# Two adaLN transformer layers on one core: statistics, normalisations, first weights and the mask of the wide attention moved

## The reference

```
mod = silu(c) @ wmod            # sa, ca, ga, sb, cb, gb: six vectors of 256 per layer
# layer 0
h = layernorm(x) * (1 + ca) + sa
x = x + ga * (softmax(q(h) k / 4) v @ Wo.T)       # 16 heads x 16, 4096 keys
h = layernorm(x) * (1 + cb) + sb
x = x + gb * experts(h)                           # 8 experts, top 2, hidden 64
# layer 1
h = layernorm(x) * (1 + ca) + sa
x = x + ga * (attention(h) @ Wproj.T + bproj)     # 16 heads x 16, 1024 keys
h = layernorm(x) * (1 + cb) + sb
h = h + causal_attention(rmsnorm(h, ln1_w)) @ wo  # 16 heads x 128
r = rmsnorm(h, ln2_w)
f = h + experts(r) + shared(r)                    # 16 experts of 176, top 6; shared 352
x = x + gb * f
```

## Time and profile before

| | |
|---|---|
| runs, us | 1858.6, 1856.21, 1847.71; median 1856.21 |
| the profiled execution, us | 1849.89, its span 1848.1 |
| TensorE busy | 1741.0 us, 94% of the span |
| VectorE busy | 1374.4 us, 74% |
| ScalarE busy | 1102.7 us, 60% |
| GpSimd busy | 517.1 us, 28% |

### The profile page before, as it was taken

The page is one execution under the profiler, slowest core; times in us unless marked ns, Lnnn a source line. Parts: engine busy times, 40 slices in busy tenths (PEclk is TensorE's granted clock), DMA queues, the critical chain, the costliest instruction groups (busy, mean ns, idle before and its releaser), DMA issues. The chain is left out here.

```text
span 1848.1 us, 29387 instructions
## 1 busy us (share of the span) xinstructions
PE 1741.0 (94%) x10457; PEld 1054.8 (57%) x10460; DVE 1374.4 (74%) x1911; ACT 1102.7 (60%) x2201; POOL 517.1 (28%) x527
## 2 busy tenths in 40 slices
PE   6999999999999999889999959999999999789997
PEld 4433333333333333564444448888888888678885
DVE  4799999999999997367999666666666666556666
ACT  2488888788788887455888425454545454244442
POOL 7247333333334522012323221110211020022223
PEclk7699999999999999999999989999999999989998
DMA  7122332223322300103546110000000000043331
GB/s 169 23 43 57 56 52 47 44 43 69 80 45 55 68 24 10 35 18 62 117 112 158 36 44 16 9 23 14 23 9 23 14 11 1 10 121 113 107 117 54
DMA packets 50606, 98.62 MB, mean 53 GB/s; under 512 B 11545, under 2 KB 21881, under 8 KB 48971
## 3 DMA queue, kind: packets, MB, share of 16 engines
q1 hardware_dynamic: 50219, 96.83, 22.0%
q10 hardware_dynamic: 288, 0.49, 0.2%
HBM read 65.63 MB, written 15.92 MB: 44 GB/s over the span
## 5 line engine op out<-in xcount | busy, mean ns | idle before, releaser
L726 DVE TENSOR_REDUCE a_max_part<-psum 128x1 f32<-128x1024 f32 x640 | 753.5, 1218 | 84.1 <-PE psum L614 82.3
L797 ACT ACTIVATE a_probs<-psum 128x512 f32<-128x512 f32 x1280 | 671.7, 600 | 186.3 <-PE psum L665 185.7
L665 PE MATMUL psum<-a_q_max,a_k_rows 51*128 51x512 f32 x1280 | 462.0, 449 | 3.4 <-ACT a_probs L797 1.8
L665 PEld LDWEIGHTS psum<-a_q_max,a_k_rows 51*128 51x128 f32 x1280 | 212.3, 187 | 354.2 <-ACT a_probs L797 286.7
L614 PE MATMUL psum<-a_k_rows,a_q_rows 48*128 48x512 f32 x1280 | 356.1, 472 | 13.7 <-DVE a_max_part L726 4.6
L654 PE MATMUL psum<-a_probs,a_v_ext 128*32 128x512 f32 x2560 | 343.3, 609 | 0.0
L614 PEld LDWEIGHTS psum<-a_k_rows,a_q_rows 48*128 48x128 f32 x1280 | 154.4, 189 | 86.7 <-DVE a_max_part L726 67.8
L1951 PE MATMUL psum<-high_t_parts,high_gu 128*128 128x512 f32 x600 | 146.4, 394 | 6.8 <-DVE high_t_parts L2045 6.8
L544 POOL TENSOR_TENSOR a_max_bf<-a_neg_max,a_zeros 128x8 bf16<-128x8 f32 x64 | 14.6, 229 | 472.5 <-issue 415.4
L417 POOL TENSOR_TENSOR a_k_rows<-a_k_in,a_k_rows 16x2048 fp32r<-16x2048 f32 x32 | 145.8, 4556 | 2.5
L1951 PEld LDWEIGHTS psum<-high_t_parts,high_gu 128*128 128x128 f32 x600 | 114.3, 191 | 31.5 <-issue 7.3
(11 more groups left out here) (223 smaller groups left out, 2139.2 us busy)
## 6 DMA issues: line engine op xcount, KB each, us to landing
o<-a_o_out SPq DMA_DIRECT2D x56, 256.0 KB, 2.2
a_k_in<-in_k SPq DMA_DIRECT2D x96, 128.0 KB, 4.6
a_q_rows<-q_high SPq DMA_DIRECT2D x124, 64.0 KB, 2.4
gu_in<-in_w_gu SPq DMA_DIRECT2D x25, 256.0 KB, 2.9
high_cw<-cw SPq DMA_DIRECT2D x24, 256.0 KB, 3.9
a_v_in<-in_v SPq DMA_DIRECT2D x16, 256.0 KB, 5.9
a_o<-o SPq DMA_DIRECT2D x8, 512.0 KB, 4.6
qk_in<-in_wqk SPq DMA_DIRECT2D x16, 256.0 KB, 2.7
```

What stands on the lines that cost most here:

```text
L665: pe.matmul(psum[:, self.bank_of(self.filling(j)), :], k_rows[rows, b, k0:k0 + P], self.q_max[rows, u % 2, :], start=True, stop=True).then ...
L726: dve.tensor_reduce(self.max_part[:, u % 2, c // self.nch, c % self.nch:c % self.nch + 1], psum[:, 2 * (n % 2):2 * (n % 2) + 2, :], AX.XY, ...
L797: act.activation(self.probs[:, p % self.pring, :], psum[:, self.bank_of(self.filling(j)), :], ACT.Exp).then_inc(self.exp_done, 1)
```

## The change

- `Attention` gets its statistics from `Merge.statistics`: behind add_out of steps 12 and 13 bn_stats of two tiles each, behind 16 to 19 of one each, into a tensor `stats` that lives through the kernel. `experts_low` does the same behind its additions. `normalise` with `stats` leaves out its bn_stats; its dummy matmuls stay.
- "n3" goes. `wide_attention` does both norms in its own block: aggregates, 16 scalar_tensor_tensor, squares with a sum on ScalarE in place of the second bn_stats, normalised tiles on VectorE (even) and ScalarE (odd), transposes, and the split parts straight from PSUM. TensorE issues 180 dummy matmuls before and 20 after the transposes.
- `WideWeights`: the first weights of the wide attention are loaded by SyncE at u = 6 and 17 of a1 and split by GpSimd at u = 13, 14, 15, 20 and 21.
- The mask is added by VectorE, in PSUM, before each maximum; the mask matmul and the bf16 casts go.
- The attention's prologue: queries and keys are sent separately (`load_q`, `load_kr`), the queries after `queries_done`; in a1 the Exp table is loaded first, and the query rows are cleared first; two value products are made ahead of the scores; 8 dummy matmuls stand on either side of `turn_maxima(0)`; in a0 75 follow the projections (`stay_busy`).
- `Front`: x is loaded before the first part of wmod; the rest of wmod waits for the first keys; 90 dummy matmuls at the start and 20 behind the column products.

The diff, cut:

```
+    def statistics(self, dve, k, stats):
+        i = k - self.PAIRS
+        tiles = (2 * i, 2 * i + 1) if 0 <= i < 2 else (i,) if i >= 4 else ()
+        for t in tiles:
+            dve.wait_ge(self.out_free, k + 1)
+            dve.bn_stats(stats[:, t, :], self.x[:, t, :]).then_inc(self.stats_done, 1)
...
                         for k in self.steps_after(u, s // 2):
                             merge.add_out(dve, k)
+                            merge.statistics(dve, k, stats)
...
             for k in range(in_slots, merge.STEPS):
                 merge.add_out(dve, k)
+                merge.statistics(dve, k, stats)
...
+                if weights is not None and u == 6:
+                    weights.load_first(sp)
+                if weights is not None and u == 17:
+                    weights.load_second(sp)
...
+                if weights is not None and u in (13, 14, 15):
+                    weights.split_first(pool, u - 13)
+                if weights is not None and u in (20, 21):
+                    weights.split_first(pool, u - 17)
...
             projection.products(pe, front)
+            if front is not None:
+                front.stay_busy(pe)
+            values_ahead = min(2, projection.tiles)
+            for t in range(values_ahead):
+                projection.value_products(pe, t)
...
+            keep_busy(pe, psum, self.ident_bf, 8)
             turn_maxima(0)
+            keep_busy(pe, psum, self.ident_bf, 8)
...
+            if not raw:
+                load_table()
+            projection.high_queries(act)
+            projection.queries_done(act)
             act.wait_ge(self.q_set, 1)
+            load_q(act, (1,), q_rows[:, 0, :], 0, self.q_loaded[0])
             if not raw:
+                projection.high_keys(act)
+                projection.chunk_done(act, 0)
                 act.wait_ge(self.k_set, 1)
...
+                load_kr(act, (1,), k_rows[:, 0, :], 0, self.q_loaded[0])
             projection.high_parts(act, 1)
+            if raw:
+                load_table()
...
-            sp.dma_start(self.wmod[:, 0, :, 0:first], by_row[0][:, :, 0:first]).then_inc(self.w_loaded[0], 16)
             for n in range(2):
                 sp.dma_start(self.x[:, 4 * n:4 * n + 4, :], x_tiles[:, 4 * n:4 * n + 4, :]).then_inc(self.x_loaded[n], 16)
+            sp.dma_start(self.wmod[:, 0, :, 0:first], by_row[0][:, :, 0:first]).then_inc(self.w_loaded[0], 16)
...
+            sp.wait_ge(attention.k_loaded, 96)
...
+            pe.wait_ge(self.ones_ready, 1)
+            keep_busy(pe, self.psum, self.ones_bf, 90)
...
+    def stay_busy(self, pe):
+        keep_busy(pe, self.psum, self.ones_bf, 75, 3)
...
+                if not made:
+                    for t in range(TT - 1):
+                        dve.bn_stats(stats[:, t, :], src[:, t, :]).then_inc(steps, 1)
+                    step(dve.bn_stats(stats[:, TT - 1, :], src[:, TT - 1, :]), TT)
...
             low(TT - 1)
+            for i in range(TT // 2 - 1):
+                statistics(i)
             add_pair(TT // 2 - 1)
-            dve.wait_ge(x_done, TT // 2)
+            statistics(TT // 2 - 1)
...
+        if n == 0:
+            pool.memset(self.zero[:, :], 0.0).then_inc(self.zero_set, 1)
+            pool.wait_ge(self.zero_set, 1)
+            pool.wait_ge(self.first_loaded, 48)
+        if n == 3:
+            pool.wait_ge(self.second_loaded, 32)
...
+        pool.tensor_tensor(parts[:, par, 0, :], src[:, :], self.zero[:, :].broadcast_to([P, size]), ALU.add).then_inc(self.high, 1)
+        pool.wait_ge(self.high, n + 1)
+        pool.tensor_tensor(parts[:, par, 1, :], src[:, :], parts[:, par, 0, :], ALU.subtract).then_inc(self.low, 1)
...
-                pe.matmul(s[:, i * P:n], id_bf[:, :], mask_bf[:, :], start=False, stop=True).then_inc(sc_full, 1)
+                mm.then_inc(sc_full, 1)
...
+            keep_busy(pe, psum, ident_bf, 180)
...
+                act.activation(junk[:, t % 2, :], x2[:, t, :], ACT.Square, accum_out=squares[:, t:t + 1]).then_inc(squared, 1)
...
+                    act.activation(t_parts[:, 0, c, half * 512:(half + 1) * 512], psum[:, 2 * c + half, :], ACT.Copy,
+                                   scale=scale_col[:, c:c + 1]).then_inc(t_hi, 1)
...
+                    last = bank_pair(i)[:, i * P:(i + 1) * P]
+                    dve.tensor_tensor(last, last, mask[:, :], ALU.add).then_inc(masked, 1)
+                    dve.wait_ge(masked, it * (2 * slots) + (slots * h + i + 1))
...
+            for t in range(TT):
+                dve.bn_aggr(mv[:, t, :], stats[:, t, :]).then_inc(steps, 1)
...
+            for t in range(0, TT, 2):
+                dve.tensor_scalar(xn[:, t, :], x2[:, t, :], rstd[:, 1, t:t + 1], None, ALU.mult).then_inc(even_ready, 1)
...
+                    dve.scalar_tensor_tensor(t_parts[:, 1, c, cut], psum[:, 2 * c + half, :], scale_col[:, c:c + 1], t_parts[:, 0, c, cut],
+                                             ALU.mult, ALU.subtract).then_inc(t_lo, 1)
...
-            dve.tensor_copy(mask_bf[:, :], mask[:, :]).then_inc(const_ready, 1)
-            dve.tensor_copy(id_bf[:, :], ident[:, :]).then_inc(const_ready, 1)
```

More of the change, by code:

```diff
@@ L456, in _, with run @@
             pool.memset(self.zeros[:, :], 0.0).then_inc(self.zeros_ready, 1)
+            self.clear_queries(pool)
             pool.memset(self.k_rows[:, :, :].bitcast(F32), 1.0).then_inc(self.k_set, 1)
             self.clear(pool)
[L460 removed]
+    def run(self, block, load_q, load_kr, q_loads, merge, projection, stats, front=None, weights=None):
         psum, nkt, nb, steps, groups, group, us = self.psum, self.nkt, self.nb, self.steps, self.groups, self.group, self.us
@@ L1075, in step, with statistics @@
                 dve.wait_ge(steps, done[0])
-            def statistics(src, rms, eps, nth):
-                for t in range(TT - 1):
-                    dve.bn_stats(stats[:, t, :], src[:, t, :]).then_inc(steps, 1)
-                step(dve.bn_stats(stats[:, TT - 1, :], src[:, TT - 1, :]), TT)
+            def statistics(src, eps):
+                if not made:
+                    for t in range(TT - 1):
+                        dve.bn_stats(stats[:, t, :], src[:, t, :]).then_inc(steps, 1)
+                    step(dve.bn_stats(stats[:, TT - 1, :], src[:, TT - 1, :]), TT)
                 for t in range(TT - 1):
@@ L2102, in adaln_two_layers @@
                     front.register(block, attention, i["c"], i["wmod"], i["ident"], i["x"], i["ln_w"], ln_w[:, :], chunks(i["wq0"]))
-                    attention.run(block, load_q, 6, merge, projection, front)
+                    attention.run(block, load_q, None, 6, merge, projection, stats, front)
         with ExitStack() as part:
```

248 lines of the change are left out of this document (155 added, 93 removed).

## The result

The changed kernel takes 1845.13 us in the median (1839.09 to 1852.63, 20 runs), the kernel before 1855.93 (1847.71 to 1861.41, 20 runs): the ratio is 0.9946, with a 95% interval of 0.9934 to 0.9957. That is 10 us by the ratio and 10.8 by the medians, a little over half a per cent, where 22 were forecast. The profiled execution of the changed kernel has a span of 1839.5 us against 1848.1, so 8.6 us less; the two profiles can be set side by side.

A forecast was written before the change was run, and what follows sets the result against it. It took TensorE to bound the loops, but not the seams between them. Terms summed to -17.3 us, 1832.6 for a profiled execution like that of before; the forecast median was 1834, 22 under that of before, range 1819 to 1851.

The forecast's parts named there:

- step 4: Narrow attention: wide weights' splits on GpSimd meet the maxima twice, 1.3 us each, plus 0.2 for loads: +2.8 (0 to +5).
- Step 1: End of first attention: moved statistics lengthen VectorE's tail by 1.75, transposes save 0.75: +1.0 us (0 to +1.8).
- the third rival: Seams: longer idle time of TensorE lets the clock fall, 1.7 us for each of two seams: 1840; chance 0.22.
- Step 2: End of the low experts: moved statistics add 1.6, transposes save 0.75: +0.85 us (-0.7 to +1.7).
- Step 3: Narrow attention's prologue: key rows come 2.3 us earlier for the first scores: -2.0 us (-2.7 to +0.5).
- Step 5: From the narrow attention's end to the wide scores: shorter norms, splits and projections: -12.4 us (-14.2 to -9).
- The -0.5 beside it: Wide attention: one table load moved out of the first slots saves 0.5 us.
- Step 6: Wide attention: mask moved from TensorE to VectorE: -7.7 saved, 1.7 charged for short slots: -6 us (-13 to +5).
- The rival that it would lie on the path: Wide attention: VectorE's mask addition and its wait delay each tile's maximum, 45 us replacing 1.7: 1877; chance 0.05.
- Step 7: Start and first attention: dummy matmuls raise the clock, x loaded before the weights' first part: -1 us (-9 to +4).
- The second rival, an early clock: First attention: the 0.53 clock of 60 to 80.3 does not recur, -6 us more: 1828; chance 0.3.

The follow-up runs named there:

- load_early: Changed kernel with SyncE's second load of the wide weights at step 15 of the narrow attention, not 17: its loop 220.90 us, ratio 0.9955 to the kernel before.
- combined_odd: Changed kernel with GpSimd's long narrow-attention operations at odd steps, second load earlier, first two statistics in normalise, 150 dummies, start tiles before modulation columns: 1825.83 us, ratio 0.9856.
- stats_in_norm: Changed kernel with the statistics of the first two normalisations taken in normalise again: ratio 0.9917 to the kernel before.
- before_again: The kernel before, profiled once more without a change: 1855.4 us, loop of the first attention 735.35 us.
- mask_on_pe: Changed kernel with the mask added by TensorE's matmul again: median 1857.0 us, ratio 1.0008 to the kernel before; wide attention 497.84 us.
- splits_odd: Changed kernel with the five weight splits at steps 13, 15, 17, 19, 21 and the second load at step 15: 1835.38 us, ratio 0.9910 to the kernel before.
- forced_overlap: Changed kernel with VectorE's four normalised start tiles held until the first keys' loads: those operations 13.26 us, first scores at 43.34 us, span 1854.8 us.
- head_as_before: Changed kernel with the old start: wmod ahead of x, its rest not held back, start's added dummy matmuls removed: 1847.12 us, ratio 0.9973 to the kernel before.
- cols_after: Changed kernel with VectorE writing its four normalised start tiles ahead of the modulation column copies: median 1844.49 us, first scores at 27.72 us.

## Why the prediction was wrong

The direction was right, the size was not: 10 to 11 us for 22. The largest part of the miss is step 4, 7 us. About 5 more of the 22 came from no step, as the prediction itself says: the steps gave -17.3 against a profiled execution that lay 6.3 under the median, and from the median the same steps give 1838.9 in place of 1834. By the steps, in the two profiles, -8.6 for -17.3:

- **Step 4, the splits in a1, failed.** It said two waits of 1.3 us at steps 14 and 20, and 0.2 for the loads. The two waits came where it said, but by luck: it held that GpSimd casts the maxima in every other step, and it casts them in each. What makes an even step dear is the late copy of the values ahead of the added work. It had no term for the two things behind these waits. GpSimd reached the split 1.83 us before its data, because SyncE's step 17 and GpSimd's step 20 fall within 3 us of each other: load_early took this off. And after a wait of TensorE in this loop the clock may fall, which here cost as much as the wait again: 1.47 us after a wait of 1.27, 3.70 after one of 3.14. combined_odd, with no waits, has neither. +9.85 for +2.8, over the +5 at which the step's range ended: 7 of the missing 9 us between -17.3 and -8.6.
- **Step 1** had the size of the tail (+1.90 for 1.75) and the saving of the transposes (2.71 to 1.92 us, 0.79 for 0.75). It left out that the 80 dummy matmuls would take 6.25 in place of 4.63: the third rival, which it held for 0.22 likely and priced at 1.7 per seam; it was 1.62. With it +3.04 for +1.0. The trace agrees here with what the Trainium skill, "TensorE: Matmul & The Clock Gate", section "HAM oscillation — how this bites in real kernels", says, that waits between bursts put the clock back: 0.73 in the 80 after the longer idle time, 1.00 before.
- **Step 2** failed in the same way: +1.34 and +0.91, so +2.25 for +0.85. The low experts between n1 and n2 took 1.31 less, which no step had foreseen: the clock was at the lower level for 6.9 us in them and for 10.3 before. Only by that luck is the sum near. stats_in_norm gives the two steps' price without the experts: 5.3 us in the profiles.
- **Step 3** was right in kind, -1.31 for -2.0: the queries' rows went out sooner, but the two value products (1.89 us) end only at 843.4. That the wait it takes away can pull the clock down behind it, 4.5 us in before_again, was not in the sum.
- **Step 5** was right in its path, and one term was mis-sized. From the last bn_stats' end to the scores the changed kernel takes 1092.49 - 1072.39 = 20.1 us, where 1081.2 - 1062.9 = 18.3 were worked out; 1.66 of the difference are the 180 dummy matmuls, which it took as hidden. The low parts came at 2.73 / 4 = 0.68 each, Square needed no table of its own. The -0.5 beside it, for the table load out of the first slots, is not there by mask_on_pe.
- **Step 6** was right, and its charge of 1.7 was not needed: the mask gave 8.0 for 6, and the pair went from 61.1 to 60.0 us. The addition costs VectorE 286 ns (122 in 34.9 us) where the earlier trace rows had 279. The rival that it would lie on the path is out. The formula of the Trainium skill, "VectorE: DVE Perf Modes", section "The TRN2 errata — SBUF-src ops pay a fixed extra latency per instruction", which the page states for longer operations, is near the duration here too (291 ns for 286), and none of it was a loss: VectorE's idle 22 us in a pair took it. The row, over 1110 to 1575 us of the changed kernel:

```profile
L1964 DVE TENSOR_TENSOR psum<-psum,wide_mask 128x128 f32<-128x128 f32 x122 | 34.9, 286 | 0.0
```

- **Step 7** can't be read from the two profiles. The loop of a0 was 731.4 to 734.5 us in eleven profiles (ten with the new start or nearly so, one with the old), 737.94 in one with the new, 738.36 and 735.35 in the kernel before. The difference of 4.5 goes with the moment at which the clock came back for good: 81.8 us in the first profile of before (738.36), 80.5 in load_early (737.94), 76.4 in the changed kernel (733.90), 64.9 in splits_odd (731.42). The second rival, an early clock, came half true: 0.68 for 0.53 in 60 to 80.3. In the mean the loop is 733.5 us in the eleven profiles without the old start and 735.9 in the three with it; with the start added, 763.4 against 763.8, as two long starts are among them (forced_overlap left out). How much the new start gives, between 0 and 5 us, stays open: the profile of head_as_before shows none, its runs 2 to 5, of which its loss at a1's start is a part.

## What to carry to other kernels

A background step that is put in another engine's idle time needs three numbers, not one: when its data land, what is queued behind it, and in which of the loop's steps that queue has slack; here the five splits cost 9.9 us in steps 13, 14, 15, 20 and 21, and nothing in 13, 15, 17, 19 and 21 with the second load two steps sooner. Where a wait of TensorE in a dense loop is costed, the clock behind it belongs to the price. Work that lay under dummy matmuls cost nothing where it was, and moving it to a tail cost its full length plus the longer idle time's effect on the clock. And one profile of a kernel is one draw: where its time is well off the median of the runs, a forecast for the median has to be counted from the median.

## What the runs showed that was not expected

- VectorE's tensor_scalar on float32 tiles in SBUF stood still while GpSimd's tensor_tensor ran: 13.26 us for four operations of 0.34 when both began together, 8.96 and 8.91 in two profiles where GpSimd began 0.64 and 0.41 us later. The Trainium skill, "SBUF — State Buffer", section "SBUF: two separate sides", says that VectorE, in operations that take both of its ports, and GpSimd share a pair of ports as an exclusive lock that the first to start holds for its whole instruction. The trace agrees that they exclude each other: three of the four operations ended 0.15 us after one of GpSimd's. Who starts first it can't tell, as VectorE's first began 0.04 us ahead of GpSimd's in forced_overlap and was still the one held. Over the profiles GpSimd's first split of keys begins at 13.8 to 15.5 us, and with the order of the changed kernel the tiles at 11.85 to 14.74, so an execution falls on one side or the other; cols_after parts them by 2 us.
- The clock fell after waits as short as 1.27 us, but not after each: the wait behind the sums was followed by an interval of 5.62 us in twelve profiles and of 8.17 in one, that behind the bias by 5.63 in twelve and 8.22 in one, and that behind the split in step 14, as long as these, by 6.99 to 7.16 in eight and 5.63 in one. Why the last so often and the others so seldom, no run shows.
- TensorE at 10.00 of 10.00 us busy ran at 0.50 in 40 to 50 us of the start, with 33 matmuls in them, where the steady loop has 625 in 99.3 us. A busy row alone does not show the upper level.
